# A routed FFN, a half-zeroed gated MLP and a routed FFN again, on one core: four expert calls in a row, another order of the prologue and first passes, and a threshold hit counted as a rank

## The chip, the cores and the metric

One Trainium2 chip, one of its cores. The metric is the device time of one execution in microseconds (us); the lower, the better. Engines are named TensorE (PE in the profile), VectorE (DVE), ScalarE (ACT), GpSimd (POOL) and SyncE (SP).

## The reference

2048 rows of 512 numbers pass three residual stages. The first and third are the same FFN with 64 experts of rank 16, 16 chosen a row; the second is a gated MLP of width 1376 in which, of each row, the 688 activations smallest in magnitude are set to zero.

```python
def ffn(xf, A, B, Wr):                       # A 64x16x512, B 64x512x16, Wr 64x512
    top_vals, top_idx = top_k(xf @ Wr.T, 16)
    G = zeros(N, 64).at[rows, top_idx].set(softmax(top_vals))
    h = einsum('nd,krd->nkr', xf, A)
    return 2.0 * einsum('nkr,kdr->nd', h * G[:, :, None], B)

def mlp(x, w_gate, w_up, w_down):
    s = silu(x @ w_gate.T)                   # 1376 wide
    _, idx = top_k(-abs(s), 688)             # the 688 smallest, of equal ones the first
    s = s.at[rows, idx].set(0.0) * (x @ w_up.T)
    return s @ w_down.T

x = x + 0.5 * ffn(layernorm(x), A, B, Wr)
x = x + mlp(layernorm(x), w_gate, w_up, w_down)
x = x + 0.5 * ffn(layernorm(x), A, B, Wr)
```

Inputs are drawn from a fixed seed.

## The kernel before

The rows are cut in NT = 16 tiles of 128. Every factor of a product is split into two float16 parts, high and low, scaled by powers of two; a product is three matmuls (high x high, low x high, high x low). Weights come in pieces: a load, `square` on ScalarE, `norms` on TensorE (a product with ones, for the scale), `make_scale` on VectorE, then `split_hi` (ScalarE) and `split_lo` (VectorE). The matrices are r (router), a and b (experts), g, u, d (gate, up, down); their staging areas overlap, so `w_u` waits for the low half of b and `w_d` for that of g (`wait_low`).

The order of every engine is written out by hand. `calls` numbers the expert calls k: (1, 0) to (1, 4) first (LEAD = 5), then in turn (1, d+5) and (3, d), where (j, t) is stage j of tile t. One call is: `norm_stats`, `rstd` (GpSimd), `norm_apply`, `x_to_hi`/`x_to_lo`, `turn_x` (a transposing DMA on the SP queue; the first two tiles are transposed by TensorE), `experts` (scores into one PSUM bank, the 1024 expert sums into banks 5 and 6), `choose` and `route` (weights of the 16 chosen), `apply_route` (reads both banks, gives `routed_ready`), `p_to_hi`/`p_to_lo`, `turn_p`, `combine`, `add_ffn`. `experts` waits with its sums until the call before has been read (`routed_ready` k).

Stage 2 of a tile: `gates` (three banks from bank 2 on), `tanh`, `silu`, `magnitude`, then a search for a threshold under which 688 of 1376 magnitudes lie. `aim` sets a first threshold `thr` from the row's sum of magnitudes and six step sizes `steps`. `count` n = 0 to 6 (ScalarE) adds up Sign(thr - magnitude) into `bal`; after counts 0 to 5 `search` (GpSimd) moves `thr`, unless |bal - 7| is under 7.5. `select` (VectorE) takes the 8 largest magnitudes at or below `thr` and picks from them the 688th smallest, `kth`. Its number is bal / 2, which holds for an even `bal` of 0 to 14. A `flag` is set when this can't be done. TensorE adds the flags of a tile over its rows (`sum_flags`); `check` loads the sum into a register, and if it is not zero the whole tile goes through `bisect`, an exact search bit by bit in 31 rounds over all magnitudes. `mask`, `v_to_hi`/`v_to_lo`, `turn_v` and `down` follow. `gated` multiplies the gate with the up projection.

In the steady loop `tile(d)` (d = 1 to FULL - 1, FULL = 11) TensorE runs `down(d)`, `combine(3, d-1)`, `gates(d+2)`, `sum_flags(d+1)`, `experts(1, d+5)`, `ups(d+2)`, `experts(3, d)`, `combine(1, d+5)`. From d = 11 on the calls of stage 1 are through. The prologue before it and the epilogue after it are straight lists.

Of the kernel before, what the change touches and what calls it, by code (L numbers as in the profile page):

```python
# [70 lines left out]
def build(nc, x, w_r, w_a, w_b, w_g, w_u, w_d, out):  # L71
# [38 lines left out]
    with ExitStack() as ctx:  # L110
# [74 lines left out]
        kth, above, wrong = col("kth"), col("above"), col("wrong")  # L185
# [6 lines left out]
        steps = sb("steps", [P, 8], F32)  # L192
        square_sums = sb("square_sums", [P, 16], F32)
# [45 lines left out]
        def squares(m, n):  # L239
# [6 lines left out]
            return place.bitcast(BF16)[0:rows, c * m.width:(c + k) * m.width]  # L246

# [27 lines left out]
        def _(sp):  # L275
# [31 lines left out]
            def turn_p(k):  # L307
# [3 lines left out]
                sp.dma_start_transpose(pt_hi[k % 2][:, :, :], p_hi[:, :]).then_inc(pt_hi_loaded, 16)  # L311
                sp.wait_ge(p_lo_ready, k + 1)
# [10 lines left out]
            def tile(d):  # L323
# [3 lines left out]
                turn_v(d + 1)  # L327
                turn_p(number[1, d + LEAD])
# [15 lines left out]
            turn_p(0)  # L344
            load_x(5)
            load_x(6)
            turn_x(1, 3)
            turn_p(1)
            turn_x(2, 0)
            turn_p(2)  # L350
            turn_x(1, 4)
# [11 lines left out]
            turn_x(2, 3)  # L363
            turn_x(1, LEAD + 1)
            load_x(SLOTS - 1)
            turn_p(number[3, 0])
# [27 lines left out]
        def _(pool):  # L394
# [19 lines left out]
            def aim(t):  # L414
# [34 lines left out]
            pool.memset(ident, 0.0).then_inc(const_made, 1)  # L449
            pool.wait_ge(const_made, 3)  # L450
# [14 lines left out]
            for n in range(len(MU.pieces)):  # L465
                if n >= 2:
                    pool.wait_ge(w_loaded["u"][n - 2], 16)
                load_w(MU, n)
            rstd(2, 0)
# [4 lines left out]
            rstd(1, 4)  # L474
# [7 lines left out]
            searches(0, 2, 3, 4, 5)  # L482
            rstd(1, LEAD)
            aim(1)
# [26 lines left out]
        def _(pe):  # L511
# [43 lines left out]
            def experts(j, t, fresh=False, norms_of=None, turn_of=None):  # L555
# [3 lines left out]
                k = number[j, t]  # L559
                x_hi = [xt_f[k % 2][:, c, :] for c in range(DC)]  # L560
# [17 lines left out]
                if k:  # L578
                    pe.wait_ge(routed_ready, k)
                if fresh:  # L580
                    for c in range(DC):
                        split_done(MA, c)
                        for o in range(2):
                            mm = three(bank(EXP + o), MA, c, slice(o * BANK, (o + 1) * BANK),
                                       x_hi[c], x_lo[c], c == 0, c == DC - 1)
                else:
                    for o in range(2):
                        for c in range(DC):
                            mm = three(bank(EXP + o), MA, c, slice(o * BANK, (o + 1) * BANK),
# [24 lines left out]
            def wide(m, t, fresh=False, flags_of=None):  # L614
# [108 lines left out]
        def _(act):  # L723
# [100 lines left out]
            for n in range(1, len(MA.pieces)):  # L824
                split_hi(MA, n)
# [583 lines left out]
```

## Time and profile before

| | us |
|---|---|
| Median of 3 runs | 881.35 |
| The three runs | 881.35, 2737.43, 881.34 |
| The profiled execution, its own time | 882.88 |
| Its span, first to last instruction | 880.7 |
| Busy in the span: TensorE | 712.3 |
| VectorE | 569.3 |
| ScalarE | 361.5 |
| GpSimd | 232.2 |
| Mean granted TensorE clock | 0.915 of full |

Busy time is of one execution, as the hardware profiler took it. Starts are counted from the span's first instruction. Names on the two sides of "<-" are tensors written and read; where a helper issues an instruction, the line is the helper's: L514 to L516 are the three matmuls of `three` (experts, gates, ups), L598, L599 and L602 those of `two_turned` (`combine`, `down`), L651 is `sum_flags`, L1155 the start of `check`, L1111 to L1150 `bisect`, L1160 the end of `check`, L1066 `silu`, L772 `count`, L790 `v_to_hi`, L421 `steps`.

### The profile page before, as it was taken

How to read it: one execution, taken by the hardware profiler on the slowest of the kernel's cores; microseconds unless marked ns; L12 is line 12 of the kernel's file. 1: busy time of each engine (PE TensorE's matmuls, PEld its weight loads, DVE VectorE, ACT ScalarE, POOL GpSimd, SP SyncE). 2: the span in 40 equal slices, each digit the busy share in tenths (PEclk: the TensorE clock that was granted, in tenths of full speed). 3: DMA queues.
4: the chain of work that ended last, by engine and by line, in shares of the span. 5: the costliest groups of instructions: out<-in, count | busy, mean ns of one | idle time of the engine just before them, and what ended most of it. 6: DMA issues, size and time to landing. Idle time of an engine off the chain costs nothing.

```text
span 880.7 us, 10845 instructions
## 1 busy us (share of the span) xinstructions
PE 712.3 (81%) x3665; PEld 334.9 (38%) x3667; DVE 569.3 (65%) x1252; ACT 361.5 (41%) x458; POOL 232.2 (26%) x618
## 2 busy tenths in 40 slices
PE   5899979799999999999999999999000006898785
PEld 2344434344545454544444444444000002444332
DVE  6788674485766657566665756655777787546542
ACT  6847843545444453535363635352000004455210
POOL 4023253324333232424241415150000003252200
PEclk9999999999999999999999999999555557999998
DMA  9485230524424352425262424231000004032231
GB/s 339 123 223 136 49 70 12 93 59 83 82 61 82 60 93 49 93 48 101 42 114 45 88 49 82 53 75 39 0 0 0 0 0 68 26 69 57 48 82 36
DMA packets 170523, 62.28 MB, mean 71 GB/s; under 512 B 163632, under 2 KB 163632, under 8 KB 170464
## 3 DMA queue, kind: packets, MB, share of 16 engines
q1 hardware_dynamic: 167952, 51.01, 28.9%
q0 software_dynamic: 2512, 10.55, 3.4%
q8 instruction: 29, 0.48, 0.2%
q14 instruction: 30, 0.25, 0.1%
HBM read 16.97 MB, written 4.19 MB: 24 GB/s over the span
## 4 chain that ended last, share of the span: by engine, by line
PE 57%; DVE 21%; issue 8%; POOL 5%; ACT 4%; DMA 3%; DVEq 1%; SPq 0%; POOLq 0%; ACTq 0%
PE ps L514 11%; PE ps L516 11%; PE ps L515 11%; PE ps L598 8%; PE ps L599 8%; PE ps L602 8%; DVE keep L1117 6%; ACT signs L772 3%; POOL small L431 1%; POOL small L429 1%; DVE mem L1137 1%; DVE mem L1086 1%; DVE small L1088 1%; DVE mem L1066 1%; DMA mem<-w_a 1%
## 5 line engine op out<-in xcount | busy, mean ns | idle before, releaser
L772 ACT ACTIVATE signs<-mem,small 128x1376 bf16<-128x1376 f32 x112 | 161.4, 1441 | 161.8 <-POOL small L431 136.8
L514 PE MATMUL ps<-w_u_hi,xt 128*128 128x512 f16 (+1 forms) x192 | 69.9, 364 | 121.1 <-DVE mem L1066 121.1
L598 PE MATMUL ps<-w_b_hi,pt_hi 128*128 128x512 f16 x256 | 98.5, 385 | 7.5 <-DMA pt_hi<-p_hi 6.4
L514 PE MATMUL ps<-w_a_hi,xt_f 128*128 128x512 f16 x256 | 100.3, 392 | 3.0 <-DVE routed L1036 2.2
L515 PE MATMUL ps<-w_a_hi,xt_f 128*128 128x512 f16 x256 | 100.0, 391 | 0.0
L516 PE MATMUL ps<-w_a_lo,xt_f 128*128 128x512 f16 x256 | 99.9, 390 | 0.0
L599 PE MATMUL ps<-w_b_lo,pt_hi 128*128 128x512 f16 x256 | 98.4, 384 | 0.0
L419 POOL TENSOR_SCALAR small<-small 128x1 f32<-128x1 f32 x16 | 22.6, 1413 | 256.8 <-ACT mem L784 236.3
L598 PE MATMUL ps<-w_d_hi,mem 128*128 128x512 f16 x176 | 68.6, 390 | 9.8 <-issue 5.5
L790 ACT ACTIVATE mem<-mem 128x1408 f16<-128x1408 f32 x16 | 22.0, 1373 | 128.1 <-DVE spare L1160 127.8
L514 PEld LDWEIGHTS ps<-w_u_hi,xt 128*128 128x128 f16 x192 | 19.1, 99 | 142.2 <-DVE mem L1066 121.8
L516 PE MATMUL ps<-w_u_lo,xt 128*128 128x512 f16 (+1 forms) x192 | 69.8, 363 | 0.0
L515 PE MATMUL ps<-w_u_hi,xt 128*128 128x512 f16 (+1 forms) x192 | 69.6, 363 | 0.0
L515 PE MATMUL ps<-w_g_hi,xt 128*128 128x512 f16 (+1 forms) x192 | 68.5, 357 | 0.0
L514 PE MATMUL ps<-w_g_hi,xt 128*128 128x512 f16 (+1 forms) x192 | 68.5, 357 | 0.0
L516 PE MATMUL ps<-w_g_lo,xt 128*128 128x512 f16 (+1 forms) x192 | 68.5, 357 | 0.0
L599 PE MATMUL ps<-w_d_lo,mem 128*128 128x512 f16 x176 | 68.4, 388 | 0.0
L427 POOL TENSOR_SCALAR small<-small 128x1 f32<-128x1 f32 x96 | 29.6, 308 | 128.6 <-ACT signs L772 127.1
L1002 DVE TENSOR_TENSOR halves<-normed,halves 128x512 f16<-128x512 f32 x30 | 20.7, 690 | 61.7 <-ACT halves L756 61.7
L602 PE MATMUL ps<-w_b_hi,pt_lo 128*128 128x512 f16 x256 | 60.5, 379 | 0.0
L1086 DVE SCALAR_TENSOR_TENSOR mem<-mem,small 128x1376 f32<-128x1376 f32 x16 | 26.4, 1651 | 51.3 <-ACT signs L772 51.3
L756 ACT ACTIVATE mem<-mem 128x512 f16<-128x512 f32 x16 | 10.1, 630 | 111.1 <-DVE mem L994 111.1
(156 smaller groups left out, 1366.5 us busy)
## 6 DMA issues: line engine op xcount, KB each, us to landing
x<-x SPq DMA_DIRECT2D x14, 256.0 KB, 2.9
out<-x SPq DMA_DIRECT2D x14, 256.0 KB, 2.3
mem<-w_g POOLq DMA_DIRECT2D x4, 688.0 KB, 8.5
mem<-w_u POOLq DMA_DIRECT2D x4, 688.0 KB, 5.6
mem<-w_d POOLq DMA_DIRECT2D x5, 512.0 KB, 5.9
mem<-w_a SPq DMA_DIRECT2D x4, 512.0 KB, 6.2
mem<-w_b POOLq DMA_DIRECT2D x4, 512.0 KB, 6.6
pt_hi<-p_hi SPq DMA_TRANSPOSE x32, 3.2
```

Source lines behind the costliest of these rows:

```text
L419: pool.tensor_scalar(thr, mag_sum, GUESS, None, ALU.mult).then_inc(thr_ready, 1)
L427: link(pool.tensor_scalar(off, bal, -7.0, None, ALU.add))
L514: pe.matmul(dst, x_hi, w_hi, start=start, stop=False)
L515: pe.matmul(dst, x_lo, w_hi, start=False, stop=False)
L516: return pe.matmul(dst, x_hi, w_lo, start=False, stop=stop)
L598: pe.matmul(dst, x_hi[:, c, :], hi[m.name][:, c, :], start=c == 0, stop=False)
L599: pe.matmul(dst, x_hi[:, c, :], lo[m.name][:, c, :], start=False, stop=False)
L602: mm = pe.matmul(dst, x_lo[:, c, :], hi[m.name][:, c, :], start=False, stop=c == chunks - 1)
L772: act.activation(signs[:, :], mags[t % 2], ACT.Sign, bias=thr, scale=-1.0, accum_out=bal).then_inc(counted, 1)
L790: act.activation(v_hi, masked, ACT.Copy).then_inc(v_hi_ready, 1)
L1086: link(dve.scalar_tensor_tensor(out=masked[:, 0:I], in0=mag, scalar=thr, in1=mag, op0=ALU.is_le, op1=ALU.mult))
L1117: dve.tensor_scalar(keep[:, :], mag, trial.bitcast(F32), None, ALU.is_lt, ALU.add, accum_out=above)
```

## The change

Five things are changed; the three matmuls of each product and their order inside a sum are not.

1. Expert calls 1 and 3 write banks 3 and 4 instead of 5 and 6. Calls 1 to 4 wait only for the call before the last; calls (1, 0) to (1, 3) now follow each other on TensorE, and (1, 4) comes before `gates(0)`.
2. The lists of the prologue are put in another order on all engines. The norms of d stand inside `gates(1)`, after its first block. `turn_p` is split in its two halves at places, with `turn_x` between them.
3. In the first passes and in `tile(1)` `check` stands elsewhere, and `sum_flags` of tiles 0 and 2 goes into the up projection, before its last block. From d = 2 on `tile` is as before.
4. `steps` is one GpSimd instruction over a constant row, `step_parts`, that six chained memsets fill at the start.
5. `select` adds 1 to `bal` when the largest candidate is equal to the threshold (`rank2`), and no longer flags that case.

No product is put in or left out to fill waits.

```diff
+        def banks_of(k):
+
+            return WIDE + 1 if k in (1, 3) else EXP
...
-                if k:
-                    pe.wait_ge(routed_ready, k)
+                if k > 1:
+                    pe.wait_ge(routed_ready, k if k > LEAD - 1 else k - 1)
...
-                for n, damp in enumerate(DAMP):
-                    link(pool.tensor_scalar(steps[:, n:n + 1], mag_sum, -SPACING / 2 * damp, None,
-                                            ALU.mult))
+                link(pool.tensor_scalar(steps[:, 0:len(DAMP)], step_parts[:, 0:len(DAMP)], mag_sum,
+                                        None, ALU.mult))
...
+            for n, damp in enumerate(DAMP):
+                link(pool.memset(step_parts[:, n:n + 1], -SPACING / 2 * damp))
...
+                    if norms_of is not None and o == BANK:
+                        norms(norms_of)
...
             experts(1, 0, fresh=True, turn_of=1)
-            experts(1, 1, norms_of=MB)
-            experts(1, 2, norms_of=MG)
+            experts(1, 1)
+            norms(MB)
+            experts(1, 2)
+            experts(1, 3)
+            norms(MG)
             combine(1, 0, fresh=True)
-            experts(1, 3)
             combine(1, 1)
             pe.wait_ge(scale_made, 4)
             norms(MU)
+            experts(1, 4)
+            pe.wait_ge(routed_ready, LEAD - 1)
             gates(0, fresh=True)
             combine(1, 2)
-            experts(1, 4)
             ups(0, fresh=True)
             combine(1, 3)
             pe.wait_ge(scale_made, 5)
-            norms(MD)
-            gates(1)
+            gates(1, norms_of=MD)
             combine(1, 4)
             pe.wait_ge(scale_made, 6)
-            ups(1)
-            sum_flags(0)
+            ups(1, flags_of=0)
             experts(1, LEAD)
...
-                sum_flags(d + 1)
+                if d > 1:
+                    sum_flags(d + 1)
                 experts(1, d + LEAD)
-                ups(d + 2)
+
+                ups(d + 2, flags_of=d + 1 if d == 1 else None)
...
+                link(dve.scalar_tensor_tensor(out=rank2, in0=cand8[:, 0:1], scalar=thr, in1=bal,
+                                              op0=ALU.is_equal, op1=ALU.add))
+                link(dve.scalar_tensor_tensor(out=top_a, in0=evens, scalar=rank2, in1=cand8,
                                               op0=ALU.is_equal, op1=ALU.mult, accum_out=kth))
...
-                link(dve.scalar_tensor_tensor(out=wrong, in0=above, scalar=2.0, in1=bal,
+                link(dve.scalar_tensor_tensor(out=wrong, in0=above, scalar=2.0, in1=rank2,
                                               op0=ALU.mult, op1=ALU.not_equal))
-                link(dve.scalar_tensor_tensor(out=wrong, in0=bal, scalar=15.0, in1=wrong,
-                                              op0=ALU.is_gt, op1=ALU.max))
                 if t:
                     dve.wait_ge(flag_summed, t)
-                dve.scalar_tensor_tensor(out=flag[:, 0:1], in0=cand8[:, 0:1], scalar=thr,
-                                         in1=wrong, op0=ALU.is_equal, op1=ALU.max
-                                         ).then_inc(flag_ready, 1)
+                dve.scalar_tensor_tensor(out=flag[:, 0:1], in0=rank2, scalar=15.0, in1=wrong,
+                                         op0=ALU.is_gt, op1=ALU.max).then_inc(flag_ready, 1)
...
             select(0)
             mask(0)
+            check(0)
             split_lo(MD, 2)
-            split_lo(MD, 3)
-            check(0)
+            v_to_lo(0)
...
             select(1)
             mask(1)
-            norm_apply(2, 3)
-            norm_apply(1, LEAD + 1)
             check(1)
```

On VectorE the first calls now run: `norm_apply(1, 2)`, `choose(0)`, `x_to_lo(1, 2)`, ..., `choose(1)`, `x_to_lo(1, 3)`, ..., `apply_route(1)`; in `tile(1)`: `add_down`, `norm_stats(3)`, `add_ffn(3)`, `norm_apply(3)`, `select(2)`, `silu(3)`, `mask(2)`, the other calls' work, `check(2)`, `p_to_lo`, `v_to_lo(2)`. On SP: `turn_p_hi(0)`, `turn_x(1, 3)`, `turn_p_lo(0)`. On ScalarE `v_to_hi(0)` stands after `count(1, 0)` (before: after `count(1, 1)`), `v_to_hi(1)` right after `count(2, 0)`. On GpSimd `rstd(1, LEAD)` stands before `search(0, 5)`, not behind it.

## Rows read from the trace of the kernel before

**Rows 1.** Windows: busy us by engine, granted clock, DMA share; two prologue stretches, one later
```profile
core 0: us, PE busy (x) PEld busy (x) DVE busy (x) ACT busy (x) POOL busy (x), PEclk, DMA share, GB/s
0.00:100.00 100.00, 85.66 (x433) 39.12 (x436) 75.30 (x179) 69.94 (x86) 28.87 (x73) 0.98 0.65 189
100.00:200.00 100.00, 87.81 (x453) 40.91 (x451) 64.49 (x120) 48.89 (x61) 33.32 (x87) 0.97 0.30 57
...
500.00:600.00 100.00, 100.00 (x523) 47.56 (x522) 61.71 (x132) 46.43 (x62) 32.96 (x88) 1.00 0.32 63
```

**Rows 2.** Windows: the stretch of the hole
```profile
611.00:733.00 122.00, 4.98 (x24) 2.04 (x21) 93.05 (x249) 0.87 (x1) 0.00 (x0) 0.53 0.00 0
```

**Rows 3.** Groups of instructions by line, 600 to 760 us: count, busy us, mean ns
```profile
L1117 DVE TENSOR_SCALAR_CACHE_REDUCE keep<-mem,ints 128x1376 f16<-128x1376 f32 x31 | 51.0, 1646 | 6.2 <-issue 6.2
```

**Rows 4.** Timeline of VectorE at 610 us and 733 us: start us, length us
```profile
610.57 0.16 DVE L1155 CAST ints<-ps 128x1 int32<-128x1 f32 x1 [0.39 <-PE ps L651]
611.51 0.06 DVE L1111 MEMSET ints<- 128x1 int32 x1 [0.79 <-DVE ints L1155]
...
733.22 1.59 DVE L1066 SCALAR_TENSOR_TENSOR mem<-mem,ps 128x1376 f32<-128x1376 f32 x1
```

**Rows 5.** Timeline of VectorE: the check of tile 9, without a fallback
```profile
482.97 0.16 DVE L1155 CAST ints<-ps 128x1 int32<-128x1 f32 x1 [1.37 <-PE ps L651]
484.40 0.06 DVE L1160 MEMSET spare<- 128x1 f32 x1 [1.27 <-issue]
```

**Rows 6.** Timeline of ScalarE: the gate activation of tile 13
```profile
610.46 1.41 ACT L779 ACTIVATE mem<-ps,small 128x1376 f32<-128x1376 f32 x1 [8.28 <-PE ps L516]
```

**Rows 7.** Timeline of TensorE after the hole: idle before, and its releaser, in brackets
```profile
734.87 0.61 PE L514 MATMUL ps<-w_u_hi,xt 128*128 128x512 f16 x1 [118.89 <-DVE mem L1066]
...
765.28 0.16 PE L651 MATMUL ps<-flag,ones 128*128 128x1 bf16 x1 [2.54 <-DVE flag L1099]
```

**Rows 8.** Timeline of TensorE: stalls of the first 190 us
```profile
27.28 0.39 PE L514 MATMUL ps<-w_a_hi,xt_f 128*128 128x512 f16 x1 [2.24 <-DVE routed L1036]
...
44.87 0.38 PE L598 MATMUL ps<-w_b_hi,pt_hi 128*128 128x512 f16 x1 [0.96 <-DVE w_b_lo L971]
...
123.92 0.59 PE L598 MATMUL ps<-w_d_hi,mem 128*128 128x512 f16 x1 [5.46 <-issue]
...
161.19 0.58 PE L598 MATMUL ps<-w_d_hi,mem 128*128 128x512 f16 x1 [3.87 <-DMA mem<-mem]
...
184.30 0.18 PE L651 MATMUL ps<-flag,ones 128*128 128x1 bf16 x1 [1.27 <-DVE x L1059]
```

**Rows 9.** Timeline of TensorE: products of one call, early and late
```profile
28.42 0.63 PE L515 MATMUL ps<-w_a_hi,xt_f 128*128 128x512 f16 x1
28.84 0.63 PE L516 MATMUL ps<-w_a_lo,xt_f 128*128 128x512 f16 x1
...
32.00 0.38 PE L516 MATMUL ps<-w_a_lo,xt_f 128*128 128x512 f16 x1
32.22 0.38 PE L514 MATMUL ps<-w_a_hi,xt_f 128*128 128x512 f16 x1
```

**Rows 10.** Timeline of VectorE: flag of tile 0, checks of tiles 0 and 1
```profile
110.38 0.22 DVE L1099 SCALAR_TENSOR_TENSOR flag<-small 128x1 bf16<-128x1 f32 x1
...
114.60 0.15 DVE L1155 CAST ints<-ps 128x1 int32<-128x1 f32 x1
...
154.92 0.15 DVE L1155 CAST ints<-ps 128x1 int32<-128x1 f32 x1
```

**Rows 11.** Timeline of ScalarE: last square of w_d, first values' high half
```profile
92.31 0.61 ACT L731 ACTIVATE mem<-mem 96x512 bf16<-96x512 f32 x1
...
118.79 1.36 ACT L790 ACTIVATE mem<-mem 128x1408 f16<-128x1408 f32 x1
```

**Rows 12.** Timeline of GpSimd: first reciprocal root, w_d loads, steps of tile 1
```profile
4.71 0.19 POOL L407 TENSOR_SCALAR rvar<-mv 128x1 f32<-128x1 f32 x1 [3.07 <-DVE mv L988]
...
59.22 1.51 POOL L401 DMA_DIRECT2D mem<-w_d  x2 [4.61 <-DVE w_g_lo L971]
...
112.33 3.58 POOL L421 TENSOR_SCALAR steps<-small 128x1 f32<-128x1 f32 x6
```

More of the change, by code:

```diff
@@ L184, in build @@
             col(n) for n in ("mag_sum", "step", "thr", "bal", "off", "far", "move"))
-        kth, above, wrong = col("kth"), col("above"), col("wrong")
+        rank2, kth, above, wrong = col("rank2"), col("kth"), col("above"), col("wrong")
         unscale_r, unscale_f, unscale_g, unscale_m = (
@@ L473, in _ @@
             load_w(MD, 1)
-            rstd(1, 4)
             rstd(2, 1)
@@ L1171, in tile @@
                 add_ffn(1, d + LEAD - 1)
-                select(d + 1)
-                mask(d + 1)
-                add_down(d)
-                norm_stats(3, d)
-                add_ffn(3, d - 1)
-                norm_apply(3, d)
-                x_to_lo(3, d)
-                check(d + 1)
-                silu(d + 2)
-                choose(k1)
-                v_to_lo(d + 1)
-                route(k1)
-                apply_route(k1)
-                norm_stats(2, d + 3)
-                if d + LEAD + 1 < NT:
-                    norm_stats(1, d + LEAD + 1)
-                p_to_lo(k1)
-                norm_apply(2, d + 3)
+                if d == 1:
+                    add_down(d)
+                    norm_stats(3, d)
+                    add_ffn(3, d - 1)
+                    norm_apply(3, d)
+                    select(d + 1)
+                    silu(d + 2)
+                    mask(d + 1)
+                    x_to_lo(3, d)
+                    norm_stats(2, d + 3)
+                    norm_stats(1, d + LEAD + 1)
+                    choose(k1)
+                    route(k1)
+                    apply_route(k1)
+                    norm_apply(2, d + 3)
+                    check(d + 1)
+                    p_to_lo(k1)
+                    v_to_lo(d + 1)
+                else:
+                    select(d + 1)
+                    mask(d + 1)
+                    add_down(d)
+                    norm_stats(3, d)
+                    add_ffn(3, d - 1)
+                    norm_apply(3, d)
+                    x_to_lo(3, d)
+                    check(d + 1)
+                    silu(d + 2)
+                    choose(k1)
+                    v_to_lo(d + 1)
+                    route(k1)
+                    apply_route(k1)
+                    norm_stats(2, d + 3)
+                    if d + LEAD + 1 < NT:
+                        norm_stats(1, d + LEAD + 1)
+                    p_to_lo(k1)
+                    norm_apply(2, d + 3)
                 x_to_lo(2, d + 3)
```

207 lines of the change are left out of this document (115 added, 92 removed).

## The prediction

> **What bounds the kernel now.** I read the execution by engine in stretches of 100 us first. From 200 to 600 us TensorE is busy without a break at its full clock, and its summed waits there are empty; between 0 and 200 us it lacks 14.3 and 12.2 us [rows 1]. So in mid-span only TensorE's own work counts, and this change leaves every product there as it is. Then the hole: between 611 and 733 us TensorE works 4.98 us of 122, VectorE 93 us, and the granted clock falls to about half [rows 2]. What VectorE does there is the fallback `bisect`: 31 times a pass over 1376 magnitudes, 1.65 us each [rows 3]. It is called when a tile's flags do not sum to zero. It runs once in 16 tiles. Counting `check` from tile 0 at 115 us on, one at the end of each tile, the one at 610.57 us belongs to tile 12 [rows 4]. TensorE meanwhile stands for 118.89 us before the up projection of tile 13, which needs that tile's gate values [rows 7].
>
> **The fallback, if it goes.** It is entered at 611.51 us, and VectorE's next work, `silu(13)`, starts at 733.22 [rows 4]. An ordinary `check` takes 1.43 us from its read of the sum to its last instruction [rows 5]; that would end this one at 612.0 us. The gate activation of tile 13, which VectorE's next instruction needs, ends at 610.46 + 1.41 = 611.87 us [rows 6], so `silu(13)` starts at about 612.0. The saving is 121.2 us. Is it all on the path? After 733 us the chain restarts from `silu(13)` and runs through VectorE, GpSimd and ScalarE (seven counts of tile 13). TensorE starts its up projection at 734.87 with matmuls of 0.61 us, cold, but by 765.28 it is waiting again, 2.54 us, for that chain's flag [rows 7], so the slow clock there was covered and gives nothing more. In the other case TensorE would finish its expert products at about 616 and start the up projection 2.4 us later after `silu` than now, warm, and be level by the end. I take 121 us, bounds 119 and 123.
>
> **Does it go?** The flag has four causes: a balance above 15, a balance below 0 or odd (no candidate matches), equal neighbours at the wanted rank, and a magnitude equal to the threshold. The profile cannot tell them apart, the inputs can. I worked the reference's gate magnitudes out in double precision, rounded them to float32 and ran the kernel's threshold steps over them with its constants. In all 2048 rows the last balance is even and within 0 to 14, so the search never ends outside its window. In tile 12 the nearest neighbours at the wanted rank are 8.4e-6 apart, relatively, but row 98 has a magnitude of 0.29780424 against a threshold of 0.29780406: 6e-7 apart, six units in the last place, balance 8. No cause but equality comes near in the tile where the fallback ran. The sum is good to some 1e-6 only (tile 10 has a pair at 4e-7 without a fallback), so this is evidence, not proof. At equality `Sign` of zero adds 0, the balance is odd, and the old code flags on two counts. The new `rank2` adds 1 exactly then: 2L - 1376 for L magnitudes at or below the threshold, which is the true even rank, here 8 or 10, well under 15. Bits do not move: banks hold the same sums in the same order, and `steps` is the same two float32 factors. So the flag of tile 12 falls to zero if `Sign(0)` is 0. `select` has as many instructions as before (one added, one dropped): nothing.
>
> What `Sign` gives at zero no row shows. Here "ScalarE activation tables: per-element evaluation and per-set limits" of the Trainium skill (section "What a function is on this engine") bears: the scaled and biased input is one fused operation, and an input of plus or minus zero gives one of a function's special results, not its curve. If the constant for `Sign` were not 0, the balance of that row would be even, `rank2` odd, and the fallback would stay; the page does not give the constant and no trace here shows it.
>
> **The first 190 us.** Four stalls of TensorE carry the argument: 2.24 us at 27.28 (second expert call waits until the first has been read from its bank), 5.46 at 123.92 and 3.87 at 161.19 (first and second down projection), 1.27 at 184.30 (the flag of tile 2, behind the second addition of `down`) [rows 8]; sum 12.84. After the first, matmuls follow each other at 0.42 us against 0.22 later [rows 9], for some 8 of them, 1.7 us; the two stalls at `down` show a first matmul of 0.59 and 0.58 us and about 7 slow ones each, 1.5 us each. Seven small stalls between 44 and 191 us, the largest 0.96 at 44.87 [rows 8], add 3.8. Everything that can be won after 24 us is thus 12.8 + 3.8 + 4.7 = 21.3 us.
>
> *Calls in a row.* Calls 1 and 3 write banks 3 and 4, so call 1 follows call 0 with no wait, at the warm clock: 2.2 + 1.7 = 3.9 us. The four calls then need `xt` 2 and 3 turned. With durations of before I get: call 1 from 24.1 to 29.6; `x_to_lo(1,2)` now stands behind `choose(0)`, 24.2, its transpose lands near 28.7; call 2 to 35.3; `x_to_lo(1,3)` 29.8, landed 33; call 3 needs `apply_route(1)`, which I place at 34.7, 0.6 us in time. VectorE is nearly full here, so up to 2 us of this may come back. On SP the half `turn_p_hi(0)` goes first and costs one issue, 1.3 us.
>
> *Weight loads.* The loads of `w_u` wait for the last piece of B's low half, which comes some 3 us earlier; its norms still make TensorE wait perhaps 1.5 us. The loads of `w_d` wait for the last low piece of the gate matrix: they start at 59.22 now [rows 12] and at about 65 then, because VectorE meets other work first. Their cover is that the norm products of `w_d` move into the gates of tile 1, about 91 us. I place the last landing near 87.
>
> *First down.* Now the flag is ready at 110.6, `check` comes at 114.60, since two `split_lo` stand before it and the sum sits behind the up projection [rows 10], and the values' high half at 118.79 [rows 11]. Then `check(0)` follows `mask(0)` at once, and the sum stands before the last block of the up projection. `norm_apply(1,5)` no longer waits for GpSimd. With TensorE 5 us ahead at the first up projection I get `check(0)` at 108.4, the high half at 110.0, landed at 115.3: 8.6 us earlier, with a stall of about 1.4 us left. *Second down.* `check(1)` is at 154.92 [rows 10], behind two `norm_apply` that wait for GpSimd. Then it comes straight after `mask(1)`, bounded by the sum in the up projection, and the stall of 3.87 with its cold start goes. *Tile d=1.* The sum moves into the up projection and `silu(3)` before `mask(2)`: 1.27 goes, and the small stall before the up projection behind it.
>
> *GpSimd.* Six chained instructions for `steps` become one; they took 3.58 us in `aim(1)` [rows 12] and hold search 0 of tile 1 until 115.9. The new one costs between 0.21 (the shortest of the old) and 1.6 us (the longest `thr`): 2.0 to 3.4 us saved there, hidden later, where TensorE bounds. Six memsets at the start, chained, cost at most the 3.6 us that six chained steps took and more likely 1.2 to 1.7; GpSimd stands idle 3.07 us before its first `rstd` [rows 12], so 0 to 0.6 us. A row shows why the range is wide: the same one-column operation takes 0.21 or 1.6 us. "SBUF — State Buffer" of the Trainium skill (section "Who interferes with whom") would say that GpSimd is held out for the length of a VectorE instruction with two SBUF inputs; by that the new instruction could lose at most one such instruction, 1.65 us [rows 3], still less than the 3.58 it replaces.
>
> Sum of the prologue: 3.9 (calls) + 4.1 + 1.5 (first down) + 3.9 + 1.5 (second) + 1.3 (d=1) + 1.6 of the small stalls = 17.8, less 1.8 for new waits that this hand schedule misses = 16 us; bounds -1 (loads of `w_d` late, below) and 21.3. Little of this is given back in mid-span: at each `check` there VectorE waits for TensorE's sum, 1.37 us in the one shown [rows 5], so its chain can follow; the price if it could not is a stall like the 1.27 us a tile. "No idle-filling products" says that none are put into the stalls that remain; the diff adds and drops no product.
>
> **Sum.** The profiled execution took 882.88 us, 2.2 outside its span of 880.7; the median of the runs shown is 881.35, 1.5 below it. 882.9 - 121 - 16 = 745.9; on the median, 744.4. One of the three runs took 2737.43 us: 1856 above the others, about 15.3 times 121, as if the other 15 tiles fell back too. Why is not to be read here; a median leaves it out.
>
> **Rivals.** *B, the fallback stays* (`Sign(0)` is not 0, near equality and not equality, or a tie): only the prologue moves, 881.35 - 16 = 865, 860 to 880. For it: the arithmetic resolves 1e-6 only. Against: nothing else in tile 12 is nearer than 8.4e-6. *C, it goes but the prologue gives little*: the late `w_d` loads. The last square of `w_d` ends at 92.9 [rows 11], 33.7 us after the first issue; if they take as long from 65, they end at 99, TensorE stands 8 us inside the gates of tile 1 and starts cold, 1.5; it decides as soon as the last square is later than 91 us, and most of the 16 is lost: 881.4 - 121 - 4 = 756. *D, slower*: C's stall while the fallback stays. The 5 us lead turns into a lag of 5, and the stalls at `down` come on top because tile 0's counts sit behind the same squares on ScalarE: 881 + 5 to 10 = 889. It needs the last square later than about 97 us, and B.
>
> **Chances.** Forecast 0.75, C 0.12, B 0.11, D 0.02. The likeliest's time is 744; its own range is 736 to 754. With C the range is 736 to 760, and it takes in the 119 to 123 of the fallback; B is left out. Two per cent, about what a measurement of this kernel can tell, is 17.6 us: the forecast and C are faster; of B a third (gains above 17.6), the rest is no change; D splits. Faster 0.91, same 0.08, slower 0.01.
>
> **What would show it.** In the profile of the changed kernel: no instruction of `bisect` and no half-clock slices near 610 us, `check(12)` followed within 2 us by `silu(13)`; calls 0 and 1 with no stall between them; the first down projection near 114 to 116 us with a stall of 1 to 2 us, the second near 147 with none; 11 to 14 us off the idle of TensorE before 190; six `steps` as one. The prediction is wrong if line `keep` appears 31 times again, or if TensorE stalls in the gates of tile 1.

## The result and the profile after

The changed kernel takes 747.74 us (median of four runs, 745.87 to 750.34), the kernel before 882.4 beside it; the ratio is 0.848, with a 95% interval of 0.844 to 0.852. The profiled execution took 747.29 us and spans 745.2. The forecast was 744, its range 736 to 760. (The kernel before had its 2737.43 us run once; 28 other executions of it lay between 880.7 and 886.6 us. What happened in that one stays open.)

In the changed file the lines have other numbers: L533 to L535 are `three`, L618, L619 and L622 `two_turned`, L554 the norms, L675 `sum_flags`, L1190 and L1195 `check`, L1101 `silu`, L1124 `select`, L799 `count`, L817 `v_to_hi`, L437 `steps`, L418 the weight loads.

The windows of after, which answer to [rows 1, 2]; columns as there:

```profile
0.00:100.00 100.00, 84.44 (x428) 38.89 (x429) 75.72 (x179) 69.00 (x85) 26.92 (x72) 0.98 0.68 186
100.00:200.00 100.00, 98.22 (x521) 47.09 (x519) 72.20 (x140) 57.47 (x75) 36.77 (x90) 1.00 0.36 70
...
611.00:733.00 122.00, 103.27 (x514) 47.66 (x511) 64.72 (x129) 47.34 (x60) 26.92 (x80) 0.95 0.25 54
```

The hole is gone; TensorE's idle fell from 12.2 to 1.8 us between 100 and 200 us, and did not fall at all between 0 and 100 (14.3 before, 15.6 now). That is already the outline of what the forecast had right and wrong.

VectorE at the end of tile 12, which answers to [rows 4]:

```profile
597.33 0.16 DVE L1190 CAST ints<-ps 128x1 int32<-128x1 f32 x1 [0.39 <-PE ps L675]
598.70 0.06 DVE L1195 MEMSET spare<- 128x1 f32 x1 [1.21 <-issue]
598.70 1.59 DVE L1101 SCALAR_TENSOR_TENSOR mem<-mem,ps 128x1376 f32<-128x1376 f32 x1
```

`silu(13)` starts 1.37 us after `check(12)` and at 598.70 instead of 733.22, 134.5 us earlier. How the two parts share this is told by the first up projection of tile 3, behind which both kernels run the same lists: it starts at 177.48 instead of 190.73. So 13.3 us come from the prologue and 121.3 from the fallback; the end follows `silu(13)` by 146.5 instead of 147.5 us, and these 1.0 us make up the 135.5 by which the span is shorter.

The stretch from the second call to that up projection, in the kernel before and then in the one after:

```profile
24.10:190.73 166.63, 149.59 (x775) 69.64 (x775) 117.29 (x239) 98.52 (x120) 46.09 (x123) 0.97 0.41 91
```

```profile
24.10:177.48 153.38, 145.54 (x776) 69.35 (x774) 115.88 (x232) 97.97 (x119) 44.41 (x109) 0.99 0.45 97
```

One line each splits the 13.3: idle went from 17.0 to 7.8 us (9.2 less), and the same products needed 149.6 and then 145.5 us (4.1 less), because fewer of them ran at the lower of TensorE's two clocks. Where the idle went is in TensorE's timeline after, which answers to [rows 8]:

```profile
24.55 0.38 PE L533 MATMUL ps<-w_a_hi,xt_f 128*128 128x512 f16 x1
...
36.07 0.19 PE L533 MATMUL ps<-w_r_hi,xt_f 128*128 128x64 f16 x1 [0.55 <-DVE scores L1049]
...
50.27 0.38 PE L618 MATMUL ps<-w_b_hi,pt_hi 128*128 128x512 f16 x1 [1.00 <-DVE x L1088]
...
61.86 0.76 PE L554 MATMUL ps<-w_d_lo,ones 128*128 128x512 bf16 x3 [4.51 <-ACT w_d_lo L762]
...
118.77 0.38 PE L618 MATMUL ps<-w_d_hi,mem 128*128 128x512 f16 x1
...
139.42 0.39 PE L533 MATMUL ps<-w_u_hi,xt 128*128 128x512 f16 x1 [1.22 <-DVE mem L1101]
...
152.68 0.38 PE L618 MATMUL ps<-w_d_hi,mem 128*128 128x512 f16 x1 [0.56 <-DMA mem<-mem]
```

Call 1 starts at 24.55 with no wait. The first down projection has no wait, the second 0.56 us. The new item is 4.51 us at 61.86, in the norms of `w_u`: TensorE waits for the last `square`. A second new one, 1.22 us at 139.42, stands before the up projection of tile 2, which waits for `silu(2)`. ScalarE and SP in that stretch, and the chain that ended last:

```profile
58.99 1.06 ACT L794 ACTIVATE p_hi<-routed 128x1024 f16<-128x1024 f32 x1 [2.66 <-DMA pt_hi<-p_hi]
59.95 0.61 ACT L783 ACTIVATE halves<-normed 128x512 f16<-128x512 f32 x1
60.47 1.33 ACT L762 ACTIVATE w_d_lo<-mem 128x1376 bf16<-128x1376 f32 x1
...
49.30 1.23 SPq L316 DMA_TRANSPOSE pt_hi<-p_hi  x1
53.64 1.23 SPq L310 DMA_TRANSPOSE xt_f<-halves  x1
54.93 3.67 SPq L324 DMA_TRANSPOSE pt_lo<-p_lo  x1
...
49.30 9.61 DMA pt_hi<-p_hi
```

The last square (60.47) stands behind `x_to_hi(2, 0)` and `p_to_hi(3)`, and the latter waits until the transposition of `p_hi` of call 2 has landed, since it overwrites what is being turned. That was issued at 49.30 and landed 9.61 us later; between 200 and 600 us the same transposition takes 3.2 us (median). At its issue two loads of `w_u`, 688 KB each, were under way: GpSimd issued the third at 48.16 and the fourth at 49.81, each as soon as the one before the last had landed. The third landed at 53.11, 3.8 us after the issue of the transposition. From then on the fourth load and the two transpositions issued at 53.64 and 54.93 shared the rest of its time, and that load was slow too: it took 9.09 us, where the three before it took 4.32, 5.39 and 4.95.

### The profile page after: what moved, and what is told of

It is laid out like the page before. It is cut to its first block, busy times and chain, and to the rows that moved or that the text cites. A ratio compares the mean times of both kernels' runs of the same rounds, so it can differ in the third digit from the quotient of the medians.

```text
span 745.2 us, 10290 instructions
## 1 busy us (share of the span) xinstructions
PE 704.2 (94%) x3667; PEld 333.7 (45%) x3667; DVE 476.1 (64%) x1003; ACT 360.8 (48%) x458; POOL 215.5 (29%) x544
## 4 chain that ended last, share of the span: by engine, by line
PE 73%; DVE 7%; ACT 5%; POOL 5%; DMA 5%; issue 4%; SPq 0%; DVEq 0%; POOLq 0%; ACTq 0%
PE ps L533 14%; PE ps L534 14%; PE ps L535 14%; PE ps L618 10%; PE ps L619 10%; PE ps L622 10%; ACT signs L799 3%; DMA pt_hi<-p_hi 2%; POOL small L447 2%; DVE mem L1122 1%; DVE small L1124 1%; DMA mem<-w_a 1%; DMA mem<-mem 1%; POOL small L445 1%; POOL small L443 1%
## 5 line engine op out<-in xcount | busy, mean ns | idle before, releaser
L799 ACT ACTIVATE signs<-mem,small 128x1376 bf16<-128x1376 f32 x112 | 161.5, 1442 | 154.9 <-POOL small L447 132.0
L618 PE MATMUL ps<-w_b_hi,pt_hi 128*128 128x512 f16 x256 | 98.3, 384 | 6.7 <-DMA pt_hi<-p_hi 5.7
L533 PE MATMUL ps<-w_a_hi,xt_f 128*128 128x512 f16 x256 | 99.7, 389 | 0.7 <-DVE w_a_lo L1006 0.7
L535 PE MATMUL ps<-w_a_lo,xt_f 128*128 128x512 f16 x256 | 99.2, 388 | 0.0
L619 PE MATMUL ps<-w_b_lo,pt_hi 128*128 128x512 f16 x256 | 98.1, 383 | 0.0
L533 PE MATMUL ps<-w_u_hi,xt 128*128 128x512 f16 (+1 forms) x192 | 69.2, 360 | 2.5 <-DVE mem L1101 2.5
L535 PE MATMUL ps<-w_u_lo,xt 128*128 128x512 f16 (+1 forms) x192 | 69.1, 360 | 0.0
L535 PE MATMUL ps<-w_g_lo,xt 128*128 128x512 f16 (+1 forms) x192 | 68.5, 357 | 0.0
L533 PE MATMUL ps<-w_g_hi,xt 128*128 128x512 f16 (+1 forms) x192 | 68.5, 357 | 0.0
L443 POOL TENSOR_SCALAR small<-small 128x1 f32<-128x1 f32 x96 | 29.3, 305 | 134.6 <-ACT signs L799 133.5
L618 PE MATMUL ps<-w_d_hi,mem 128*128 128x512 f16 x176 | 66.7, 379 | 1.5 <-DMA mem<-mem 1.5
L619 PE MATMUL ps<-w_d_lo,mem 128*128 128x512 f16 x176 | 66.7, 379 | 0.0
L622 PE MATMUL ps<-w_b_hi,pt_lo 128*128 128x512 f16 x256 | 60.5, 379 | 0.0
L436 POOL TENSOR_SCALAR small<-small 128x1 f32<-128x1 f32 x16 | 21.2, 1325 | 130.6 <-ACT mem L811 113.6
L424 POOL TENSOR_SCALAR rvar<-mv 128x1 f32<-128x1 f32 x48 | 11.4, 238 | 154.3 <-DVE mv L1023 152.6
L447 POOL TENSOR_SCALAR small<-small,steps 128x1 f32<-128x1 f32 x96 | 49.4, 514 | 10.8 <-POOL small L445 0.2
```

What stands on the lines that cost most here:

```text
L436: pool.tensor_scalar(thr, mag_sum, GUESS, None, ALU.mult).then_inc(thr_ready, 1)
L443: link(pool.tensor_scalar(off, bal, -7.0, None, ALU.add))
L447: pool.tensor_scalar(thr, move, steps[:, n:n + 1], thr, ALU.mult, ALU.add).then_inc(thr_ready, 1)
L533: pe.matmul(dst, x_hi, w_hi, start=start, stop=False)
L535: return pe.matmul(dst, x_hi, w_lo, start=False, stop=stop)
L618: pe.matmul(dst, x_hi[:, c, :], hi[m.name][:, c, :], start=c == 0, stop=False)
```

## The experiments

Times are medians, but for e3 and e9, which were measured once. Batch 1 (e1 to e4) stands beside 882.95 us for the kernel before, batch 2 (e0, e5, e6, e8) beside 882.66, batch 3 (e7, e9 to e11) beside 883.14. The changed kernel itself was run again in batches 2 and 3.

**e1: only the new `select`, in the kernel before.**

```diff
+ link(dve.scalar_tensor_tensor(out=rank2, in0=cand8[:, 0:1], scalar=thr, in1=bal,
+                               op0=ALU.is_equal, op1=ALU.add))
... bal -> rank2 in the three instructions behind it, the old equality flag dropped
```

> The kernel before with the new select alone (rank2), all else as it was. My theory (the fallback of tile 12 comes from a magnitude equal to the threshold, and Sign of zero adds 0): no bisect, silu(13) at 612.0 us instead of 733.2, stalls of the first 190 us unchanged (5.46 and 3.87 us at the down projections), 882.4 - 121 = 761 us. Rival B (near, not equal, or Sign(0) is not 0, or a tie): one bisect in tile 12, 882 us. Both together with the rest of the change are then additive if this saves 120 to 123 of the 135 us.

Measured: 762.07 us (760.73 to 763.74), ratio 0.863 [0.860, 0.865]. VectorE at tile 12:

```profile
611.28 0.16 DVE L1154 CAST ints<-ps 128x1 int32<-128x1 f32 x1 [0.39 <-PE ps L651]
612.65 0.06 DVE L1159 MEMSET spare<- 128x1 f32 x1 [1.21 <-issue]
```

The fallback alone is 882.95 - 762.07 = 120.9 us. And as the flags of tile 12 sum to zero with nothing changed but `rank2`, the cause was equality, and `Sign` of zero adds 0: had it added 1 or -1, `bal` would be even there, `rank2` odd, and the flag set. The prediction found the constant for `Sign` missing in the Trainium skill, "ScalarE activation tables: per-element evaluation and per-set limits" (section "What a function is on this engine"); this run answers it. TensorE's stalls at the two down projections stay as in [rows 8], 5.46 and 3.88 us.

**e2: the reverse, the changed kernel with the old `select`.**

```diff
- in0=evens, scalar=rank2 ... in0=above, scalar=2.0, in1=rank2
+ in0=evens, scalar=bal ... in0=above, scalar=2.0, in1=bal
+ ... in0=cand8[:, 0:1], scalar=thr, in1=wrong, op0=ALU.is_equal, op1=ALU.max
```

> The changed kernel with the old select and its flag. Theory: bisect is back once, in tile 12, TensorE stands some 119 us before the up projection of tile 13, and the rest keeps its 13 us: 747.7 + 121 = 869 us. Rival (the new order alone removes the flag, since a sum of magnitudes or a step differs in its last bit): no bisect, 748 us.

Measured: 870.05 us (868.23 to 871.9), ratio 0.986 [0.982, 0.989]. The fallback is back in tile 12, from 599.44 us on, with the same 31 passes as [rows 3]:

```profile
L1153 DVE TENSOR_SCALAR_CACHE_REDUCE keep<-mem,ints 128x1376 f16<-128x1376 f32 x31 | 51.0, 1646 | 6.2 <-issue 6.2
```

So the prologue alone gives 882.95 - 870.05 = 12.9 us; with 120.9 it adds up to 133.8, against 882.4 - 747.74 = 134.7. The two parts don't interact.

**e3: the kernel before, its first threshold nudged.** Only where the searches start is moved, so the threshold of row 98 ends at another value.

```diff
-GUESS = 5.7715e-4
+GUESS = 5.7716e-4
```

> The kernel before with the first threshold a hair higher (GUESS 5.7716e-4 instead of 5.7715e-4, a change of the search's start, not of what is computed). Theory of a coincidence: the equality of one row in 2048 is gone, no bisect, 761 us, with a chance of one in ten of another row meeting its threshold elsewhere. Rival (tile 12 holds a row that the search or a tie can't settle): bisect stays in tile 12 at 611 us, 882 us.

Measured once: 761.04 us, no `bisect` in the trace. One step in the fifth digit of a starting value is worth 121 us: the fallback was a coincidence of one value, not a property of tile 12, and by its arithmetic `rank2` takes care of an equality wherever it occurs (e1 is the one run that shows it, in tile 12).

**e4: the changed order, but every call in banks 5 and 6 and waiting for the call before.**

```diff
-            return WIDE + 1 if k in (1, 3) else EXP
+            return EXP
...
-                if k > 1:
-                    pe.wait_ge(routed_ready, k if k > LEAD - 1 else k - 1)
+                if k:
+                    pe.wait_ge(routed_ready, k)
```

> The changed kernel, but all expert calls write banks 5 and 6 again and each waits until the call before has been read. Theory: call 1 waits for apply_route(0), now at 25.5 us, so a stall of 2.2 us near 24.5 and some 8 cold products (1.7 us), and calls 2 and 3 wait for apply_route(1) and (2) too, which stand later on VectorE than before (35.8 and 45.1 us): calls 3 and combine(1,0) slip by some 4 to 8 us. But TensorE waits 4.5 us at 61.9 for the squares of w_u anyway, and that wait absorbs part: 747.7 + 3 to 6 = 751 to 754 us. Rival (the wait for w_u hides all of it): within 1 us of 747.7.

Measured: 755.8 us (753.66 to 760.01), ratio 0.857 [0.853, 0.861], 5.3 to 8.1 above the three medians of the changed kernel. TensorE:

```profile
26.54 0.39 PE L533 MATMUL ps<-w_a_hi,xt_f 128*128 128x512 f16 x1 [1.83 <-DVE routed L1071]
...
36.76 0.61 PE L533 MATMUL ps<-w_a_hi,xt_f 128*128 128x512 f16 x1 [4.41 <-DVE routed L1071]
...
46.20 0.39 PE L533 MATMUL ps<-w_a_hi,xt_f 128*128 128x512 f16 x1 [1.04 <-DVE routed L1071]
...
68.53 0.75 PE L554 MATMUL ps<-w_d_lo,ones 128*128 128x512 bf16 x3 [1.39 <-ACT w_d_lo L762]
```

Three waits, 7.3 us together, where the order before has one of 2.24: in the new order there is no other work between the calls to hide them. 3.1 us come back in the norms of `w_u`. And the first sign of what makes that wait: `p_hi` of call 2 is turned only at 59.08 here, after the loads have landed (the last at 56.82) and with no other transposition beside it, and takes 3.0 us.

**e0 and e10: the changed kernel again.**

> The changed kernel once more, as the level for the runs beside it: 748 us, up projection of tile 3 at 177.5 us, the span from one execution to another within 4 us, most of it in the first 60 us where loads land.

> The changed kernel once more, five rounds, beside e11. 749.5 us, single executions from 746 to 754. In the profile the stall at the norms of w_u is anything between 3 and 9 us, and the slow products behind TensorE's waits in the last three tiles cost between 5 and 10 us; the two together make the spread.

Measured: 750.47 us (747.68 to 753.38), ratio 0.850 [0.847, 0.853], and 749.12 (746.75 to 754.45), 0.849 [0.846, 0.852]. All three ratios agree. Executions of this one kernel are up to 8.6 us apart, and the wait in the norms of `w_u` differs between profiled ones: 4.51, 2.98 and 8.01 us. I collected it from the profiled executions in which `p_to_hi(3)` stands ahead of the last square and both the last load of `w_u` and this transposition are in flight together as above (us); e4 (3.0 and 1.39) and e9 (4.7 and 5.69) have another order of transfers and another difference, and are left out:

| execution | transposition of `p_hi`, call 2 | wait in the norms of `w_u` | difference |
|---|---|---|---|
| e0 | 8.09 | 2.98 | 5.11 |
| changed kernel, first | 9.61 | 4.51 | 5.10 |
| e2 | 11.54 | 6.44 | 5.10 |
| e7 | 11.70 | 6.60 | 5.10 |
| e8 | 12.45 | 7.34 | 5.11 |
| e10 | 13.11 | 8.01 | 5.10 |
| e5 | 13.66 | 8.55 | 5.11 |

In these seven, whatever the transposition takes beyond 5.1 us, TensorE stands. The last load of `w_u` lands within 0.2 us of it in each, so the table alone can't tell which of the two sets the wait; e6 and e11, below, ask that. The two rows of e10, chain and TensorE:

```profile
47.80 13.11 DMA pt_hi<-p_hi
...
63.88 1.33 PE L554 MATMUL ps<-w_d_lo,ones 128*128 128x512 bf16 x3 [8.01 <-ACT w_d_lo L762]
```

**e6 and e11: the last square of `w_u` ahead of `p_to_hi(3)`.**

```diff
+            square(MU, 3)
             p_to_hi(3)
             x_to_hi(2, 0)
-            square(MU, 3)
```

> The changed kernel with one line moved: ScalarE squares the last piece of w_u before p_to_hi(3) and x_to_hi(2,0), not after. In the changed kernel TensorE stands 4.51 us at 61.86 for that square and then runs cold; ScalarE waited 2.66 us there, for the transpose of p_hi(2) that was issued at 49.3. Theory (ScalarE's order behind a late transpose makes the stall): the square runs at about 58, the stall falls to 1.5 to 2.5 us, the cold start behind it shrinks, up projection of tile 3 some 2 to 3 us earlier, 745 us. Rival (the load of w_u itself is late, or gates(0) waits for the low half of the gate matrix instead): stall or a new one of the same size, 748 us.

> e6 once more, five rounds: the last square of w_u before p_to_hi(3). Theory: the stall at the norms stays under 2.5 us in every execution, whenever the transpose of p_hi(2) lands, so the median is 1 to 3 us under that of the changed kernel beside it and the highest execution is lower. Rival (p_to_hi(3) and the low half of the gate matrix take the stall over in gates(0)): same median within 1 us.

Measured: 750.55 us (747.82 to 751.29), 0.849 [0.847, 0.852], against 750.47 of the control, and 749.97 (747.58 to 751.1), 0.849 [0.847, 0.851], against 749.12. No gain in the median. TensorE in e6:

```profile
59.59 0.75 PE L554 MATMUL ps<-w_d_lo,ones 128*128 128x512 bf16 x3 [1.29 <-ACT w_d_lo L762]
...
68.84 0.38 PE L533 MATMUL ps<-w_g_hi,xt 128*128 128x512 f16 x1 [0.75 <-DVE w_g_lo L1006]
...
80.38 0.39 PE L533 MATMUL ps<-w_u_hi,xt 128*128 128x512 f16 x1 [1.18 <-DVE mem L1101]
```

The wait shrinks to 1.29 us, and two others come: for the low half of `w_g`, and before the first up projection. In e11 the last load of `w_u` itself took 9.29 us from its issue, so the square had nothing to read before 60.04, and 3.11 us of wait stayed. The wait is bounded by the transfers, not by ScalarE's order alone. A pair of executions whose transposition took the same time says how much the order is worth: in e6 (8.05 us) the up projection of tile 3 starts 125.8 us after the issue of that transposition (176.04 and 50.25), in e0 (8.09 us) 126.0 us (175.12 and 49.10).

**e9: the same loads with one under way at a time instead of two.**

```diff
-                if n >= 2:
-                    pool.wait_ge(w_loaded["u"][n - 2], 16)
+                if n >= 1:
+                    pool.wait_ge(w_loaded["u"][n - 1], 16)
```

> The changed kernel with the four loads of w_u one after the other (each waits for the one before, not for the last but one). Theory (the transposes issued from 49 us on, p_hi(2) above all with 7 to 14 us to landing against a median of 3.2, share the DMA engines with two outstanding loads of w_u): with one outstanding, p_hi(2) lands in at most 7 us, but the last piece of w_u comes 1 to 3 us later, so TensorE's stall at the norms of w_u is 3 to 5 us all the same; 750 us. Rival (the transposes are slow by themselves, being issued three in a row): p_hi(2) lands as late as before, stall 5 to 9 us, 753 us.

Measured once: 753.68 us. The answer on transfers shows

```profile
pt_hi<-p_hi SPq DMA_TRANSPOSE x1, 4.7
```

so beside one load and no other transposition it takes 4.7 us, and beside neither 3.0 (e4). What makes 8.1 to 13.7 of it is only in part told by this. Two loads alone don't: in the kernel before `p_lo` of call 1 was turned at 47.08, beside two loads of `w_u` from its issue to its landing and with no other transposition, and the answer on transfers there shows

```profile
pt_lo<-p_lo SPq DMA_TRANSPOSE x1, 6.9
```

(7.0 in e1 and 6.9 in e3, with the same order.)

Nor do transpositions in a row, the rival: in the changed kernel five of them, issued at 184.25 to 190.36 with no weight load beside them, took 3.0 to 3.9 us each. In the executions of the table two loads stand beside the first 3.7 to 4.4 us, and then one load with two further transpositions. And e9 takes away both things at once, since the next transposition is issued only at 61.56. So that the loads stretch the transposition is shown; how the rest divides between the second load and the transpositions behind is not. As a cure it fails: the last load is now issued at 57.73 instead of some 50, `rstd` of x(1, 4) stands behind it on GpSimd (58.34 instead of about 50.4), and TensorE waits three times at the norms:

```profile
61.72 1.33 PE L554 MATMUL ps<-w_d_lo,ones 128*128 128x512 bf16 x3 [5.69 <-ACT w_d_lo L762]
64.29 1.33 PE L554 MATMUL ps<-w_d_lo,ones 128*128 128x512 bf16 x3 [1.25 <-ACT w_d_lo L762]
67.00 1.33 PE L554 MATMUL ps<-w_d_lo,ones 128*128 128x512 bf16 x3 [1.38 <-ACT w_d_lo L762]
```

**e7: the checks of tiles 0 and 1 where they stood before**, behind two `split_lo`, and behind two `norm_apply`.

```diff
             mask(0)
-            check(0)
             split_lo(MD, 2)
+            split_lo(MD, 3)
+            check(0)
...
             mask(1)
+            norm_apply(2, 3)
+            norm_apply(1, LEAD + 1)
             check(1)
```

> The changed kernel with check(0) again behind two split_lo of w_d and check(1) again behind two norm_apply. Theory (the earlier checks close the stalls at the down projections): check(0) 2.5 us later than 111.8, so the first down projection waits about 2 us where it now waits for nothing; check(1) some 1 to 5 us later (its two norm_apply wait for GpSimd, which does aim(2) first), so the second waits 2 to 5 us more, with a cold start of 1.5 us. Second down 4 to 6 us later, 753 to 756 us beside a level of 749 to 750. Rival (the lead that the order brought elsewhere is all, the checks had slack): 750 us.

Measured: 754.22 us (753.16 to 757.79), 0.854 [0.852, 0.855], 5.1 above e10. TensorE waits again at both down projections:

```profile
124.42 0.38 PE L618 MATMUL ps<-w_d_hi,mem 128*128 128x512 f16 x1 [1.89 <-issue]
...
160.04 0.58 PE L618 MATMUL ps<-w_d_hi,mem 128*128 128x512 f16 x1 [3.66 <-DMA mem<-mem]
```

**e8: `tile(1)` in its old order, all else changed.**

```diff
-                if d > 1:
+                if d > 0:
                     sum_flags(d + 1)
...
-                if d == 1:
+                if d == 0:
                     add_down(d)
... (d = 0 does not occur: turn_p, v_to_hi and x_to_hi in the same way)
```

> The changed kernel with tile(1) in the order of before on all engines (sum of flags after the gates, select and mask ahead of the addition of down, silu late). Theory: the stalls of 1.27 us (flag of tile 2) and 0.64 us (up projection of tile 3) come back, up projection of tile 3 at 179 to 180 instead of 177.5, 750 us. As TensorE now comes 11 us earlier to this place and the search of tile 2 only some 9, the stall may be larger than before, up to 4 us: 752. Rival (the lead gained earlier makes it moot): 748 us.

Measured: 757.06 us (756.06 to 760.17), 0.858 [0.855, 0.861], 6.6 above e0; more than I expected. The wait of 1.27 us in [rows 8] has become

```profile
180.02 0.19 PE L675 MATMUL ps<-flag,ones 128*128 128x1 bf16 x1 [4.52 <-DVE x L1094]
```

TensorE now gets there earlier, but `add_down` and what VectorE does ahead of the flag do not: the time saved before the second down projection is only kept if the order of this tile goes with it.

**e5: six instructions for `steps` as before.**

```diff
-                link(pool.tensor_scalar(steps[:, 0:len(DAMP)], step_parts[:, 0:len(DAMP)], mag_sum,
-                                        None, ALU.mult))
+                for n, damp in enumerate(DAMP):
+                    link(pool.tensor_scalar(steps[:, n:n + 1], mag_sum, -SPACING / 2 * damp, None,
+                                            ALU.mult))
```

> The changed kernel with the six chained steps instructions back. Theory: aim(1) again holds search(1,0) for about 2 us, tile 1's counts and so silu(2) and the second down projection slip by 0 to 2 us; in mid-span nothing. 748 to 750 us. Rival (GpSimd's search sets the pace of the last tiles, where TensorE waits for flags, so six steps cost 1 us a tile there): 751 us.

Measured: 751.44 us (746.71 to 753.44), 0.850 [0.847, 0.854], against 750.47: no difference that can be measured. GpSimd in e5, then in the changed kernel:

```profile
115.48 2.59 POOL L438 TENSOR_SCALAR steps<-small 128x1 f32<-128x1 f32 x6
118.15 0.21 POOL L444 TENSOR_SCALAR small<-small 128x1 f32<-128x1 f32 x1
```

```profile
111.83 0.33 POOL L437 TENSOR_SCALAR steps<-step_parts,small 128x6 f32<-128x6 f32 x1
113.59 0.95 POOL L443 TENSOR_SCALAR small<-small 128x1 f32<-128x1 f32 x1 [1.43 <-ACT signs L799]
...
115.03 1.39 POOL L445 TENSOR_TENSOR small<-small 128x1 f32<-128x1 f32 x1
116.53 2.29 POOL L447 TENSOR_SCALAR small<-small,steps 128x1 f32<-128x1 f32 x1
```

VectorE beside the last four of these rows, in the changed kernel:

```profile
113.18 1.28 DVE L1006 SCALAR_TENSOR_TENSOR w_d_lo<-mem,small,w_d_hi 128x1024 f16<-128x1024 f32 x1
114.73 1.64 DVE L1201 TENSOR_TENSOR mem<-mem 128x1408 f16<-128x1408 f32 x1 [0.27 <-ACT mem L817]
116.30 3.14 DVE L1006 SCALAR_TENSOR_TENSOR w_d_lo<-mem,small,w_d_hi 128x1024 f16<-128x1024 f32 x3
```

The six take 2.59 us and the one 0.33, but search 0 of tile 1 then waits 1.43 us for the count, and its four instructions, 1.03 us long in sum in the kernel before (0.19 to 0.34 each), take 4.9 here (0.31 to 2.29). They take 4.6 in e5 too, so the shorter `steps` did not make them long. The rows show what did: the long ones begin while VectorE runs an instruction with two inputs in SBUF, and end just behind it (114.54 behind 114.47, 116.42 behind 116.37, and 116.53 + 2.29 = 118.82 behind 118.78, the end of the second of the three, with no gap between the first and the second). In the changed kernel each of the 40 one-column operations of GpSimd over 0.8 us begins while such an instruction is under way. Two of the six `steps` of [rows 12] did as well (1.22 and 1.11 us), so a good part of their 3.58 us was VectorE's. From the start of `aim` to the end of search 0 it is 6.6 us in the kernel before, 9.1 in e5 and 8.4 here: the one instruction gives 0.7 us, while the search behind it, now beside `split_lo` and `v_to_lo`, is 3.9 us longer in its four instructions than in the kernel before.

## Why the prediction was right, and where it was off

**The fallback** (121, bounds 119 to 123): right. The trace gives 121.3, e1 120.9. `check(12)` is followed after 1.37 us by `silu(13)`, as forecast; that the cold matmuls behind the hole gave nothing more holds within the 1.0 us of the last stretch. Rival B was decided by the argument about odd and even balances, and e1 to e3 confirm each link of it: equality, `Sign` of zero, one unlucky value.

**The prologue** (16, bounds -1 to 21.3): 13.3 in the trace, 12.9 by e2. Idle fell by 9.2 us instead of the 11 to 14 forecast, the clock gave 4.1 instead of 4.7. By steps, from where each phase of TensorE starts in the two traces:

| step | forecast | measured |
|---|---|---|
| start of the first up projection: calls in a row and small stalls, less new waits | 5 earlier | 0.9 later |
| the same at the second up projection | 5 earlier still | 0.5 later |
| first down, stall and slow restart | 5.6 | 7.1 (5.6 by its start, 118.77 for 123.92 from a start 0.47 late, and 1.4 by its end, its products at full clock) |
| up projection of tile 2 | nothing | 1.4 lost (the new stall of 1.22 at 139.42) |
| second down | 5.4 | 5.7 (3.3 by its start, 152.68 for 161.19, and 2.4 more by the next phase: its products run at full clock, and a stall of 0.66 behind them is gone) |
| tile d=1 with the stall ahead of the up projection | 1.3 and part of 1.6 | 2.3 |

So the sum came close in part by luck: the first 106 us gave nothing where 5 us had been counted on, and the first down projection gave 1.5 us more than forecast because TensorE reached it late. The lead of 5 us was also more than the terms of the sum hold up to there, 3.9 + 1.6 - 1.8 = 3.7.

**The step that failed** is "its norms still make TensorE wait perhaps 1.5 us". It measured 4.51 us and 2.98 to 8.55 in others, and some seven products behind it stood 0.43 us apart instead of 0.22. Together this gives back all that the calls in a row had won. The table of e0 and e10 shows how the landing of the transposition sets this wait, to a hundredth of a microsecond. I had ordered SP's issues but given each transposition its usual 3.2 us; the new order turns `p_hi` of call 2 with two loads of `w_u` in flight and two more transpositions behind it. "DMA: Bandwidth & Descriptors" of the Trainium skill (section "Issuing engines are not separate DMA queues") says that transfers of the scalar, sync and gpsimd engines run on the same 16 DMA engines and interleave; the traces agree (3.0 us beside nothing, 4.7 beside one load, 6.9 beside two, 8.1 to 13.7 in the changed order). It is a mis-sized term of a sum whose mechanism held: the 3.9 us for the calls in a row were there (call 1 starts at 24.55 for 27.28 and, at full clock, its sums end at 29.73 for 34.16), and e4 shows the second pair of banks to be worth 5.3 to 8.1 us in this order.

**First down**: forecast `check(0)` 108.4, high half 110.0, landed 115.3, a stall of 1.4 left. Measured 111.82, 113.34, and no stall, since TensorE arrived at 118.77 and not at 114. Here two misses met: all of VectorE's times shifted with the missing lead, and ScalarE's `count(1, 0)` first waited 1.70 us for GpSimd's threshold. The stall is gone for a worse reason than early values. **Second down**: forecast near 147 with no stall, measured 152.68 with 0.56; the 5.7 us are the missing lead. e7 shows the places of the two checks to be worth 5.1 us, e8 the order of `tile(1)` 6.6, not 1.3: I had priced it by the stall that the old order shows, which is what remains of it while TensorE is late there anyway.

**`steps`**: 2.0 to 3.4 us saved in the instruction itself, as forecast (2.3 to 3.3 by e5 and [rows 12]), but only 0.7 us of it reached the end of the search behind, and nothing that can be measured the time. The reason the forecast gave for its range, a wait for a VectorE instruction with two inputs in SBUF, is in the rows of e5; its bound of one such instruction is not: L447 was held over two, for 2.29 us. Nor did the forecast ask what its own move of VectorE's `split_lo` and `v_to_lo` would do to GpSimd's search.

**Rival C** was false for a reason that I gave only in part. The `w_d` loads started at 69.72, later than my 65; the last square began at 91.53 and ended by 92.24, against my 87 for the landing. But TensorE reached the norms at 96.53, not at 91. With the 5 us lead, and the squares no earlier, it would have waited about a microsecond there (an estimate, 92.2 less 91): the cover was thinner than I said.

**The tail**: `silu(13)` to the end took 146.5 us here; across executions the stretch from the flag sum of tile 13 on takes 114.7 us in the changed kernel's first profile and 119.8 in e0. In both, the same stalls stand there (0.9 to 5.9 us each, 20.2 and 21.4 in sum); 27 and 46 products at about 0.43 us stand behind them, 5.5 and 9.5 us more than at full clock. With the wait of the norms that accounts for most of the difference between the profiled executions; what decides how many there are stays open.

## What to carry to other kernels

A fallback that runs for a whole tile is a lottery on the data: find which of its conditions fired from the inputs, then remove the false one; one flag here cost nine times what all the reordering of the prologue gave. Stalls in a hand-ordered list are not additive: one that looks like 1.3 us grows to 4.5 as soon as the engine gets there earlier, and a lead won early is lost at the next transfer that comes due. When steps move, price each transfer by what else is in flight at its new place, not by its usual length, and each GpSimd operation by what VectorE runs beside it.

## What had not been expected of the hardware

- One transposition of a 128x1024 half (SP's queue) took 3.0 us alone, 4.7 beside one 688 KB load, 6.9 beside two, and 8.1 to 13.7 where two loads, then one load and two further transpositions stood beside it; the lengths differ between executions of one program. The load beside it took 7.7 to 13.2 us instead of 4.2 to 6.2. SP's own issue of the third transposition in a row took 3.67 us (7.32 in e10) instead of 1.23, and ended 0.3 us before the first one landed (0.45 in e10).
- `Sign` of zero adds 0 to the sum of a ScalarE activation.
- GpSimd's operation in one line (L447 of the changed kernel) takes 2.29 us at 116.53, where the kernel before needed 0.34 at 116.98. All 40 over 0.8 us begin under a VectorE instruction with two inputs in SBUF, and 26 of them end within 0.1 us of the end of one; no run moved such an instruction away to try it.
- The number of matmuls at the lower clock behind the same stalls differed between executions (27 to 46 from the flag sum of tile 13 on), which is worth 4 us.
